# The head of an attention kernel in another order: norms, first projections, stacking and weight loads

## The reference, cut to what matters

```
x = x + LN(attention(LN(x)))
x = x + LN(lora_ffn(LN(x)))

attention: q = x @ wq            # 32 heads of 32
           k = x @ wk, v = x @ wv  # one key and one value head for all
           softmax(causal(q k^T / sqrt(32))) v, then @ wo
lora_ffn:  8 experts of rank 16, weighted by 8 * softmax(x Wr^T + br)
           2 * sum_h score_h * B_h (A_h x)
```

## Time and profile before

| what | value |
| --- | --- |
| median of three runs | 3582.85 us (3578.75 to 3583.64) |
| the profiled execution | 3581.36 us |
| its span | 3579.6 us |
| busy share PE, DVE, ACT, POOL | 92%, 64%, 44%, 59% |
| mean granted TensorE clock | 0.966 of full |

### The profile page before, as it was taken

How to read it: one execution, slowest core, us unless ns; L and a number is a source line. 1 busy time by engine, 2 the same in 40 slices (tenths; PEclk the granted TensorE clock), 3 DMA queues, 4 the chain that set the end, 5 groups by cost and what they waited for, 6 DMA issues and landing times.

```text
span 3579.6 us, 45027 instructions
## 1 busy us (share of the span) xinstructions
PE 3306.6 (92%) x15784; PEld 1612.1 (45%) x15784; DVE 2299.5 (64%) x5996; ACT 1567.7 (44%) x3121; POOL 2121.2 (59%) x773
## 2 busy tenths in 40 slices
PE   5789998999999999999987999999999999999897
PEld 3344444444444444443444444444445444444333
DVE  3557776767777767764355667667777676666605
ACT  1233344444454545455422234444445454445552
POOL 0234666756756777876423256766666667776870
PEclk8899999999999999999998899999999999999998
DMA  3312111101110100101111121111111010000000
GB/s 84 122 49 71 41 48 36 54 28 42 34 36 16 60 22 28 33 22 31 60 48 48 36 66 42 48 37 53 28 39 36 22 30 28 27 27 24 31 1 24
DMA packets 132897, 144.00 MB, mean 40 GB/s; under 512 B 28088, under 2 KB 93624, under 8 KB 132672
## 3 DMA queue, kind: packets, MB, share of 16 engines
q1 hardware_dynamic: 132672, 141.13, 13.5%
HBM read 72.91 MB, written 16.78 MB: 25 GB/s over the span
## 4 chain that ended last, share of the span: by engine, by line
PE 57%; POOL 21%; DVE 10%; issue 5%; ACT 5%; SPq 2%; DMA 1%; POOLq 0%; ACTq 0%; DVEq 0%
POOL ds L597 15%; PE ps L1232 10%; PE ps L1250 10%; PE ps L1341 9%; PE ps L1220 8%; PE ps L1206 8%; DVE mx L869 4%; POOL ds L594 3%; ACT pr L672 2%; PE ps L1259 2%; PE ps L1281 2%; SPq L493 1%; POOL xr L614 1%; PE ps L1370 1%; PE ps L1382 1%
## 5 line engine op out<-in xcount | busy, mean ns | idle before, releaser
L672 ACT ACTIVATE pr<-ps 128x512 f32<-128x512 f32 (+3 forms) x2560 | 1304.6, 533 | 1546.9 <-PE ps L1232 1032.0
L597 POOL TENSOR_TENSOR ds<-ds,pr 128x2048 f32<-128x2048 f32 (+1 forms) x376 | 1518.7, 4039 | 207.1 <-ACT pr L672 179.0
L1232 PE MATMUL ps<-qs,ks 98*128 98x512 f32 (+3 forms) x2560 | 1366.8, 539 | 83.8 <-ACT pr L672 67.0
L869 DVE TENSOR_REDUCE mx<-ps 128x1 f32<-128x512 f32 x1536 | 996.8, 682 | 438.0 <-PE ps L1220 432.8
L1220 PE MATMUL ps<-ks,qs 96*128 96x512 f32 (+3 forms) x2560 | 969.8, 389 | 53.9 <-DMA qs<-q 27.1
L1232 PEld LDWEIGHTS ps<-qs,ks 98*128 98x128 f32 x2560 | 490.7, 192 | 776.7 <-ACT pr L672 497.8
L866 DVE CUSTOM_DVE_ANT_0 ps<-ps,mask_qk 128x128 f32<-128x128 f32 (+3 forms) x1024 | 492.0, 497 | 447.2 <-PE ps L1220 443.2
L1220 PEld LDWEIGHTS ps<-ks,qs 96*128 96x128 f32 x2560 | 498.9, 197 | 287.1 <-issue 135.5
L1250 PE MATMUL ps<-pr,vs 128*32 128x512 f32 (+3 forms) x5120 | 616.6, 554 | 7.0 <-POOL pr L604 6.8
L1206 PE MATMUL ps<-xT,wq_sb 128*128 128x512 f32 x1024 | 525.6, 614 | 13.7 <-DVE ks L930 10.3
L1341 PE MATMUL ps<-wo_sb,ao 128*128 128x512 f32 x896 | 461.5, 613 | 24.1 <-DVE q L858 24.1
(11 more groups left out here) (147 smaller groups left out, 1967.8 us busy)
## 6 DMA issues: line engine op xcount, KB each, us to landing
qs<-q SPq DMA_DIRECT2D x768, 64.0 KB, 2.0
wq_sb<-in_L_attn_wq_dram SPq DMA_DIRECT2D x64, 512.0 KB, 4.3
t<-in_L_attn_x_dram SPq DMA_DIRECT2D x32, 512.0 KB, 6.7
xr<-in_L_attn_x_dram SPq DMA_DIRECT2D x28, 512.0 KB, 3.6
out_dram<-xr SPq DMA_DIRECT2D x28, 512.0 KB, 2.6
qs<-mT SPq DMA_DIRECT2D x256, 4.0 KB
wo_sb<-in_L_attn_wo_dram SPq DMA_DIRECT2D x1, 4096.0 KB, 14.0
xT<-in_L_attn_x_dram SPq DMA_DIRECT2D x4, 512.0 KB, 5.1
```

The costliest lines, as they stand in the source:

```text
L597: nc.gpsimd.tensor_tensor(ds[:, :, c0:], ds[:, :, c0:], this, ALU.add).then_inc(added, 1)
L672: nc.scalar.activation(pr[:, k % NS, g, c0:], ps[:, PST + head(n, t, g) % NPS, c0:], ACT.Exp, scale=SCALE).then_inc(exp_done, 1)
L869: nc.vector.tensor_reduce(found, seen, AX.X, ALU.max).then_inc(mx_done, 1)
L1232: last = nc.tensor.matmul(ps[:, bank, c0:], ks[0:STK + 2, c:c + P], qs[0:STK + 2, n % NS, g, c0:], start=True, stop=not by_mask)
```

## The change

The loop from unit 4 on stays as it is. In the head and in the first units:

- One Newton chain for the four tiles together: two instructions to start, three rounds of three on 128x4 operands, one instruction for minus mean times r. The norms of tiles 1 and 3 go to ScalarE, those of 0 and 2 stay on VectorE, ahead of the copies. ScalarE does one small exponential first.
- Queries of unit 0 come first, keys and values second, in another PSUM bank (`PPV`), so neither waits for the other's evacuation. The copy of keys and values lies in a buffer of the probabilities (`pr`).
- The stacking of unit 0 is issued half by SP, half by ScalarE. ScalarE also issues the rows of unit 0.
- Queries of unit 1 are projected between the maxima of unit 0, and five of eight products of unit 2 ahead of the loop. The head does 16 maxima; the other 8 of unit 1 and the first 8 of unit 2 are spread over slots 2 to 15 of unit 0.
- The tokens of block 1 load at slot 7 of unit 0 (after the stacking of unit 2), the FFN weights at slot 8 of unit 1, wo at slot 8 of unit 3. The transposes of the FFN weights move two slots later in unit 2. The statistics of block 1 lie in units 1 to 3.

```diff
     def goal(n, j):
         k, every = j + 1 + slots(n) // 2, slots(n)
+        if n == 0:
+            return head(1) + max(0, (j - 1) * (slots(1) + slots(2) // 2) // (every - 2))
...
-    FIRST_GOAL = head(1) + slots(1) // 2
+    FIRST_GOAL = head(1)
+    Q2 = 5
...
-                for k in range(KT):
+                for k in range(Q2 if m == 2 else 0, KT):
                     at(64 * u + first + apart * k // 2, "PE", "q", m, k)
...
-                at(64 * 2 + 5 * i, "PE", "wt", i)
-                at(64 * 2 + 5 * i, "DVE", "wt", i)
+                at(64 * 2 + 8 + 5 * i, "PE", "wt", i)
+                at(64 * 2 + 8 + 5 * i, "DVE", "wt", i)
+            at(64 + 32, "SP", "ffn")
+            at(64 * 3 + 32, "SP", "wo")
...
-        at(4, "SP", "tokens", blk)
+        at(28 if blk == 1 else 4, "SP", "tokens", blk)
         for i in range(TB):
+            t0 = 64 + 48 * i if blk == 1 else 64 * i + 42
...
+            load_wq(0)
             (key and value weights)
-            load_wq(0)
             load_wq(1)
-            stack(0)
+            stack(0, range(GH // 2))
             load_wq(2)
             stack(1)
             load_wq(3)
-            rows(0)
-            (FFN weights, wo)
...
+            def first_norm(i):                       # ScalarE
+                act.wait_ge(head_nb, 1)
+                nc.scalar.activation(t4[:, i, :], t4[:, i, :], ACT.Identity, scale=LN["pre"]["r"][:, i:i + 1],
+                                     bias=nb[:, i:i + 1]).then_inc(x0n_act, 1)
+            def first_stack():
+                act.wait_ge(q1_sb, 1)
+                act.wait_ge(q2_sb, 1)
+                for g in range(GH // 2, GH):
+                    for row, part in ((0, q1), (HD, q1), (2 * HD, q2)):
+                        act.dma_start(qs[row:row + HD, 0, g, :].bitcast(F32), ...)
...
+            for i in (1, 3):
+                first_norm(i)
             for i in range(TB):
                 turned(0, i)
+            project(0)
+            first_stack()
             key_values(0)
-            project(0)
             project(1)
             rows(0)
+            first_rows()
...
+            def first_rsqrt():                       # VectorE, 128x4 operands
+                then(nc.vector.tensor_scalar(w, var, EPS, 0.5, ALU.add, ALU.mult))
+                then(nc.vector.tensor_scalar(y0, w.bitcast(I32), -0.5, float(MAGIC), ALU.mult, ALU.add))
+                for k in range(ROUNDS):
+                    then(nc.vector.tensor_tensor(a, y, w, ALU.mult))
+                    then(nc.vector.tensor_tensor(a, a, y, ALU.mult))
+                    then(nc.vector.scalar_tensor_tensor(out=y_next, in0=a, scalar=-1.5, in1=y, ...))
+                nc.vector.scalar_tensor_tensor(out=nb[:, :], in0=mean, scalar=-1.0, in1=r, ...).then_inc(head_nb, 1)
...
-            for i in range(TB):
-                rsqrt("pre", i, i, i + 1)
-            for i in range(TB):
-                token_norm(0, i)
+            first_rsqrt()
+            for i in (0, 2):
+                first_norm(i)
+            for i in range(TB):
                 turned(0, i)
+            project(0)
             key_values(0)
-            project(0)
-            project(1)
-            value_turn(0)
             for m in range(FIRST_GOAL):
                 maximum(*ITEMS[m])
+                if m == 3:
+                    value_turn(0)
+                elif m == 14:
+                    project(1)
...
             for k in range(KT):                      # TensorE
-                key_values(0, k)
-            value_turn(0)
-            for k in range(KT):
                 project(0, k)
             for k in range(KT):
+                key_values(0, k)
+            for k in range(2):
                 project(1, k)
             for m in range(FIRST_GOAL):
                 max_scores(*ITEMS[m])
+                if m == 1:
+                    value_turn(0)
+                elif m % 2 and m < 14:
+                    project(1, (m + 1) // 2)
             max_rows(0)
+            for k in range(Q2):
+                project(2, k)
```

More of the change, by code:

```diff
@@ L406, in bass_mqa_sandwich_lora_router, with kv_of, kv_bank @@
         t_stored = sem("tail_stored")
+        head_rsqrt = sem("head_rsqrt")
+        head_nb = sem("head_nb")
+        x0n_act = sem("x0n_act")
+        x0n_dve = sem("x0n_dve")
+        def kv_of(blk):
+            return kv_room if blk else kv_first
+        def kv_bank(blk):
+            return PX if blk else PPV
         block = ctx.enter_context(nc.Block())
@@ L428, in shared_bank @@
         def shared_bank():
-            order = [("kv", 0), ("q", 0), ("q", 1)]
+            order = [("q", 0), ("q", 1), ("q", 2)]
             for n in range(UN):
@@ L484, in load_wq, with stack @@
                 sp.dma_start(wq_sb[:, n % NW, :, :], wq_v[:, :, n % NU * P:(n % NU + 1) * P]).then_inc(wq_loaded[n % NW], 16)
-            def stack(n):
+            def stack(n, heads=range(GH)):
                 sp.wait_ge(q1_sb, n + 1)
@@ L490, in stack @@
                     sp.wait_ge(st_ready, head(n - NS + 1))
-                for g in range(GH):
+                for g in heads:
                     for row, part in ((0, q1), (HD, q1), (2 * HD, q2)):
@@ L511, in store, with ffn_weights @@
                 sp.dma_start(out_t[j], xr[:, j % 2, :]).then_inc(stored[j % 2], 16)
+            def ffn_weights():
+                sp.dma_start(zs[:, 0, :], ffn_a.rearrange("h r d -> (h r) d")).then_inc(wt_loaded, 16)
+                sp.dma_start(zs[0:NF, 1, :], ffn_wr).then_inc(wt_loaded, 16)
+                sp.dma_start(br_sb[:, :], ffn_br.partition_broadcast(P)).then_inc(wt_loaded, 16)
+                for n in range(D // P):
+                    sp.dma_start(xr[:, 0, n * P:(n + 1) * P].rearrange("p (h r) -> p h r", h=NF),
+                                 fb_v[n]).then_inc(wt_loaded, 16)
             load_tokens(0)
+            load_wq(0)
             for c in range(3):
@@ L650, in _, with first_rows @@
             act.wait_ge(pool_const, POOL_CONST)
+            nc.scalar.activation(slT[:, 0:HD], ones[:, :], ACT.Exp)
+            def first_norm(i):
[7 more added lines that the diff above has]
+                    for row, part in ((0, q1), (HD, q1), (2 * HD, q2)):
+                        act.dma_start(qs[row:row + HD, 0, g, :].bitcast(F32),
+                                      part[g * HD:(g + 1) * HD, :].bitcast(F32)).then_inc(qs_loaded[0], 16)
+            def first_rows():
+                act.wait_ge(mt_sb, 1)
+                for g in range(GH):
+                    act.dma_start(qs[STK:STK + 2, 0, g, :].bitcast(F32),
+                                  mT[2 * g:2 * g + 2, :].bitcast(F32)).then_inc(qm_loaded[0], 16)
             def project(n):
@@ L825, in rsqrt @@
                 L = LN[kind]
-                s, base, done = L["s_ch"], CH * n, [0]
+                s, base, done = L["s_ch"], CH * (n - TB if kind == "pre" else n), [0]
                 here = range(CH) if part is None else range(2 * part, 2 * part + 2)
@@ L849, in rooted, with then @@
             def rooted(kind, n):
-                dve.wait_ge(LN[kind]["s_ch"], CH * (n + 1))
+                dve.wait_ge(LN[kind]["s_ch"], CH * (n + 1 - (TB if kind == "pre" else 0)))
+            def first_rsqrt():
+                L, done = LN["pre"], [0]
+                w, y0, r, mean, var = L["w"][:, :], L["y0"][:, :], L["r"][:, :], L["mv"][:, :, 0], L["mv"][:, :, 1]
+                def then(ins):
+                    done[0] += 1
+                    ins.then_inc(head_rsqrt, 1)
+                    dve.wait_ge(head_rsqrt, done[0])
+                dve.wait_ge(L["s_mv"], TB)
+                then(nc.vector.tensor_scalar(w, var, EPS, 0.5, ALU.add, ALU.mult))
+                then(nc.vector.tensor_scalar(y0, w.bitcast(I32), -0.5, float(MAGIC), ALU.mult, ALU.add))
+                y = y0.bitcast(F32)
+                for k in range(ROUNDS):
+                    a, y_next = L["a"][:, k, :], r if k == ROUNDS - 1 else L["y"][:, k, :]
+                    then(nc.vector.tensor_tensor(a, y, w, ALU.mult))
+                    then(nc.vector.tensor_tensor(a, a, y, ALU.mult))
+                    then(nc.vector.scalar_tensor_tensor(out=y_next, in0=a, scalar=-1.5, in1=y, op0=ALU.add, op1=ALU.mult))
+                    y = y_next
+                nc.vector.scalar_tensor_tensor(out=nb[:, :], in0=mean, scalar=-1.0, in1=r, op0=ALU.mult,
+                                               op1=ALU.mult).then_inc(head_nb, 1)
             def project(n):
@@ L855, in project @@
                     dve.wait_ge(qs_loaded[(n - 1) % NS], stacked(n - 1))
-                if n % NU == 0:
+                if n and n % NU == 0:
                     dve.wait_ge(v_tr, n // NU + 1)
@@ L1301, in key_values @@
                     pe.wait_ge(xt_dve, TB * (blk + 1))
-                last = nc.tensor.matmul(ps[:, PX, :], wkv_sb[:, k, :], xT[:, k, :], start=(k == 0), stop=(k == KT - 1))
```

(3 more changed lines are left out.)

40 lines of the change are left out of this document (26 added, 14 removed).

## The result

| kernel | median of the runs | lowest to highest | profiled execution | its span | mean granted clock |
|---|---|---|---|---|---|
| before | 3584.09 us (6 runs) | 3578.75 to 3590.13 | 3581.36 | 3579.6 | 0.966 |
| changed | 3544.12 us (6 runs) | 3535.79 to 3551.30 | 3543.98 | 3542.2 | 0.968 |

The changed kernel takes 0.989 of the time before, with an interval of 0.9873 to 0.9907: 1.1% faster. The forecast was 3541 (3531 to 3553) with "faster" at 0.94. The forecast lead was 41.6 us, and the two spans differ by 3579.6 - 3542.2 = 37.4.

A forecast was written before the change was run, and what follows sets the result against it. The chain was taken as mostly TensorE's (57%), the head as single steps. 3581.36 less 41.6 (chain 5.4, norms 5.7, queries/keys order with split stacking 11.5, maxima 3.0, unit 0 16) gives 3539.8, median 3541; range 3531 to 3553.

The forecast's parts named there:

- Newton chain and norms: Head: first projection starts at 21.75 instead of 32.87; the chain saves 5.4 us, the norms 5.7.
- Queries first: Head: queries of unit 0 take 7.8 us, are done at 29.55, and their stacking starts at 31.0.
- Stacking and keys beside each other: Head: stacking lands at 36.25, keys ready at 38.8; first max scores then instead of 61.37, 22.6 us ahead.
- Rival 1: Head: ScalarE as second issuer shares the pace of SP; about 5 us, 3546; chance 0.10.
- Maxima with the projection of unit 1 between them: Head: rows issued at 51.2, loop starts at 54.9, 25.6 us ahead; five products of unit 2, 4.3 us, hidden.
- rival 2: Head and early slots: TensorE runs at half pace; about 7 us, 3548; chance 0.10.
- Unit 0: Wait for unit 2's stacking 2.2 us instead of 15.6; unit 1 starts at 83.3 instead of 124.95.
- Moved loads: Units 1 to 4: FFN loads hidden, wo costs 0 to +2 us, FFN transposes -1 to +1.5, taken as 0.
- rival 3: First units: FFN 8.3, wo 11 and tokens 5 us in front of rows, none given back; 3565; chance 0.08.
- From there on the difference should stand at 41 to 42 to the end: From unit 1's first scores near 83.3 on, the lead stays at 41 to 42 us to the end.
- rival 4: Whole kernel slower: a dip of TensorE's clock lasts longer or recurs; six such stretches give 3592; chance 0.04.
- rival 5: After the head: the lead is absorbed by a wait that does not move with the start; 3583; chance 0.02.

The follow-up runs named there:

- the run with one queue: All stacking and the rows of unit 0 issued by SP alone, against the changed kernel: 3557.57 us.
- the last group: Timed on one chip beside the kernel before: changed 3542.00 us; wo in slices 3543.71; plus earlier FFN transposes, later tokens 3538.70; plus norms on VectorE 3547.55.
- both pairs: Four norms on VectorE against the changed kernel: 3552.49 to 3543.98 us; against wo in slices, earlier FFN transposes, later tokens: 3547.55 to 3538.70.

## Why the prediction was right, and what was off

The mechanism held: the lead is made before unit 1, of the parts named, and the rest follows it. Step by step:

- **Newton chain and norms.** First projection forecast at 21.75, measured 21.13. ScalarE's norms took 1.2 each and TensorE's wait is for VectorE's, as forecast. That they are worth having was not asked: with four norms on VectorE the first projection starts at 20.4 and 20.6, with two on ScalarE at 20.5 to 21.4.
- **Queries first.** Forecast 7.8 us, measured 7.10: full pace, so the reserve for half pace was not needed. Stacking issued at 29.67, forecast 31.0.
- **Stacking and keys beside each other.** Right in full. ScalarE's six issues took 4.09 us and SP's 3.78, from the same moment; the first score was released by the keys at 37.39 (38.8). The Trainium skill, "DMA: Bandwidth & Descriptors", section "Issuing engines are not separate DMA queues", says that a second issuer saves only the issue time, and calls that usually small beside the DMA itself. The trace agrees with the first; here the issue time, 0.63 us each, added up to 7.0 us of the loop's start and 10.2 of unit 1's in the run with one queue, since other DMAs stood in that one's way. Rival 1 is refuted.
- **Maxima with the projection of unit 1 between them.** Rows issued at 49.53 (51.2), loop at 54.32 (54.9). The prediction put five products of unit 2 into the wait for the rows, 4.3 us and all hidden. They are the ten matmuls from 48.73 on, two to a product. They took 6.15 us, at a granted clock of 0.70 from 48.7 to 51 and 0.69 from there to 54.3, and no DMA releases the first scores. In the changed kernel's trace from the last group the same ten ran at full pace, and the scores came no earlier:

```profile
48.77 4.46 PE L1282 MATMUL ps<-xT,wq_sb 128*128 128x512 f32 x10
...
54.23 0.50 PE L1308 MATMUL ps<-qs,ks 98*128 98x512 f32 x1 [1.00 <-DMA qs<-mT]
```

  So the half pace, rival 2 on the spot, cost 0.1 us here. What the prediction had too small is the way from the rows' issue to the first scores, 3.67 by SP's rows before and 4.8 now: ScalarE's four issues took 3.23 us where SP's took 2.52.
- **Unit 0.** It now does all sixteen maxima of unit 1 and eight of unit 2, the 24 that the prediction counts; the list of the change names only eight of unit 1. Unit 2's stacking issued at 64.08 (67.0), waited for 1.90 us (2.2), unit 1 at 81.86 (83.3). The two runs on the loads show that this needs both parts: with the loads in front the wait is 14.72; with the loads moved but the old head it is 9.65. The rows of unit 1 behind the tokens were forecast to be "just in time". They have no margin: in the other two traces of the changed kernel unit 1 starts at 81.65 and 83.06, the latter after a wait of 2.23 for these rows instead of 0.65.
- **Moved loads.** Here a term was mis-sized. FFN in unit 1 was hidden, as said. Of wo the prediction said that the rows of unit 4 land 1.5 later and "the 1.5 is given back: 0, to +2". They did come later, by 4.7 - 3.6 = 1.1 us. The DMA view of 137 to 154 us (KB each, us to landing) has the reason, wo needs 14.5 us from 137.56 on, to 152.1, and the rows come with its end:

```profile
wo_sb<-in_L_attn_wo_dram SPq DMA_DIRECT2D x1, 4096.0 KB, 14.5
```

  The wait was given back as forecast: the stacking that TensorE waited 1.67 for, 10 us later, is no longer waited for. The time was not. From the slice in unit 3 to that in unit 5 it took 47.44 us before, 49.7 to 51.4 in the seven traces with wo whole ahead of those rows, and 47.4 to 48.2 in the six with wo in slices or in the head. The step cost 2.3 to 3.9 us instead of 0 to 2, and since the waits together had become shorter, it is TensorE's half pace behind the wait for the rows, of which the prediction had not thought. The transposes cost about +1.5, the top of their range. With both, the moved loads were paid for with 4 to 5 us of the 24 of rival 3, though not by its mechanism, long waits, alone.
- **"From there on the difference should stand at 41 to 42 to the end"** failed. It stood at 43.1, 39.0, 44.1, 34.4 and 36.9. A first part is wo. The rest lies in units that the change doesn't touch, goes in both directions with the granted clock there, and is in part that of the one trace of the kernel before. It isn't a drift, so it is not rival 4 (the mean clock is 0.968, before 0.966). Nor was the lead absorbed (rival 5).

The forecast of 41.6 thus met 43.1 at unit 1, less 3.7 at unit 4, less 2.0 of the clock's ups and downs by the end: 37.4 between the two profiled executions. Between medians it is 40.0 in the first set of runs and 42.6 in the second. The mechanism was right; that the time came within 3 us of the forecast is in part luck, for the terms erred in both directions: 1.5 us more at unit 1, 3.7 less around unit 4, and two more from the clock.

What stays open: why the kernels with four norms on VectorE lose 9 us by the end, in both pairs, although their head is no longer. The rows show that it is TensorE's granted clock, in unchanged work; they don't show what in the head decides it. The shared Newton chain, the queries ahead of the keys, and the maxima moved into unit 0 were not undone one by one: what each is worth is read from the timelines. A version with wo right behind `load_wq(3)`, alone and without the other loads, was not tried.

## What to carry to other kernels

A long wait for a small transfer has three cures: nothing large in front of it in its queue, an earlier issue, a later first use. Here the first alone left 9.65 of 15.64 us, the new head without it 14.72, and all together 1.90. When a large load is moved away from one such place, look for the next small transfer behind it in the queue, and don't price a longer wait of TensorE at its length: 1.1 us more cost 2.3 to 3.9, because half pace came behind it. And a gain in the head is to be read at the first point where both kernels run the same code again; at the end of a long kernel the granted clock adds some us in either direction, which is not the edit's.

## What the runs showed of the hardware

- SP issues as fast beside ScalarE as alone: 0.63 us a DMA of 64 KB in both. ScalarE took 0.68 us for one of 64 KB, and 0.81 for one of 4 KB where SP takes 0.63. No run shows ScalarE issuing alone, so whether SP slows it is not known.
- TensorE's granted clock of 0.50 after the wait of 1.94 us lasted 8 us and more (154 to 162 above); after a wait of 0.87 at the same place it stayed at 1.00. Whether it falls is not fixed by the wait alone. Behind the same wait of 1.90 for unit 2's stacking it was 0.57 from 73 to 77 us in the changed kernel's first trace, and 1.00 from 74.3 to 78.3 in the one from the last group.
- One and the same kernel, wo in slices, had a lead of 39.8 in one trace and 33.2 in another at the last wq slice. Executions of the kernel before follow their mean granted clock: 3579.22 us at 0.967, 3584.61 at 0.964, 3590.84 at 0.962. The changed kernel's ten timed runs go from 3535.79 to 3551.30. So a difference of 5 us of a single execution of this kernel says nothing, and the waits of 1 to 3 us that were removed could not be seen in its time, only in its stretches.
